# Causal attention on one core: the fourth key block of a chunk's diagonal joins the second one's tile of scores

## The reference, cut to what matters

```
def _L0_attn_ref(x, Wq, Wk, Wv, Wo, bo):        # x: (4, 2048, 256), 16 heads of 16
    q, k, v = split_heads(x @ Wq), split_heads(x @ Wk), split_heads(x @ Wv)
    scores = jnp.einsum('bhqd,bhkd->bhqk', q, k) * HEAD ** (-0.5)
    scores = jnp.where(causal, scores, -jnp.inf)
    weights = jax.nn.softmax(scores, axis=-1)
    out = jnp.einsum('bhqk,bhkd->bhqd', weights, v)
    return out.transpose(0, 2, 1, 3).reshape(B, S, N_EMBD) @ Wo + bo

x = x + _L0_attn_ref(_layernorm(x), ...)
x = x + _L0_ffn_ref(_layernorm(x), L0_ffn_rhs)   # rows quantised to int8, one 256x256 product
```

## Time and profile before

| | before |
|---|---|
| median of 3 executions | 1966.17 us (1963.51 to 1981.74) |
| profiled execution | 1967.51 us, span 1965.7 us |
| mean granted TensorE clock | 0.944 of full speed |
| PE busy | 1746.4 us, 89% of the span |
| DVE busy | 1503.5 us, 76% |
| ACT busy | 1406.9 us, 72% |
| POOL busy | 339.6 us, 17% |

### The profile page before, as it was taken

One profiled execution on the slowest core, in us unless ns is written; L12 is line 12 of the kernel. 1 busy time (PEld: TensorE's weight loads), 2 busy tenths in 40 slices (PEclk: granted clock), 3 DMA queues, 4 the chain that ended last, 5 costly groups with the idle time before them and its releaser, 6 DMA issues. The chain is left out here.

```text
span 1965.7 us, 43129 instructions
## 1 busy us (share of the span) xinstructions
PE 1746.4 (89%) x17855; PEld 676.0 (34%) x17855; DVE 1503.5 (76%) x1761; ACT 1406.9 (72%) x2915; POOL 339.6 (17%) x379
## 2 busy tenths in 40 slices
PE   5888888999999899999999999999999998887773
PEld 3444442333333333333333333333233332225442
DVE  3546558999979798988989798989789894106776
ACT  2222226888978888888888898888788888874443
POOL 7212210101010111111110101011111111013443
PEclk9989998999999999999999999999899998887876
DMA  3333220111110101010111111010101010403661
GB/s 100 123 107 105 84 68 22 29 31 41 29 38 21 43 16 43 23 36 30 29 30 38 34 30 42 16 43 16 43 28 30 30 29 19 141 18 105 187 203 63
DMA packets 102492, 106.36 MB, mean 54 GB/s; under 512 B 19092, under 2 KB 85912, under 8 KB 102296
## 3 DMA queue, kind: packets, MB, share of 16 engines
q1 hardware_dynamic: 102296, 103.60, 17.6%
HBM read 60.56 MB, written 42.47 MB: 52 GB/s over the span
## 5 line engine op out<-in xcount | busy, mean ns | idle before, releaser
L915 ACT ACTIVATE prob<-psum 128x512 f32<-128x512 f32 (+3 forms) x2560 | 1224.2, 532 | 214.0 <-PE psum L822 171.6
L346 DVE TENSOR_REDUCE pmax<-psum 128x2 f32<-128x1024 f32 (+1 forms) x960 | 1107.0, 1215 | 165.1 <-PE psum L259 128.0
L842 PE MATMUL psum<-prob,V 128*32 128x256 f32 (+1 forms) x10240 | 752.6, 367 | 9.9 <-ACT ust L904 7.2
L822 PE MATMUL psum<-Q,K 50*128 50x512 f16 (+3 forms) x2560 | 465.6, 359 | 50.9 <-ACT prob L915 40.9
L931 POOL TENSOR_SCALAR_AFFINE_SELECT prob<-prob 128x512 f32<-128x512 f32 x256 | 162.9, 636 | 1322.0 <-ACT prob L915 1322.0
L842 PEld LDWEIGHTS psum<-prob,V 128*32 128x32 f32 x10240 | 204.5, 109 | 331.2 <-issue 259.2
L259 PE MATMUL psum<-K,Q 48*128 48x512 f16 x1536 | 301.7, 395 | 13.2 <-DMA K<-k_parts 8.4
L822 PEld LDWEIGHTS psum<-Q,K 50*128 50x128 f16 x2560 | 125.7, 93 | 304.9 <-ACT prob L915 275.7
L259 PEld LDWEIGHTS psum<-K,Q 48*128 48x128 f16 x1536 | 72.3, 93 | 283.6 <-issue 159.7
L346 DVE TENSOR_REDUCE pblk<-psum 128x8 f32<-128x1024 f32 x128 | 152.2, 1217 | 8.9 <-PE psum L278 8.4
L278 PE MATMUL psum<-K,Q 48*128 48x512 f16 (+3 forms) x1024 | 126.8, 300 | 0.0
(11 more groups left out here) (104 smaller groups left out, 741.0 us busy)
## 6 DMA issues: line engine op xcount, KB each, us to landing
f_x<-in_L_attn_x SPq DMA_DIRECT2D x32, 512.0 KB, 3.9
unnormalised<-ust SPq DMA_DIRECT2D x64, 256.0 KB, 3.1
q_parts<-part SPq DMA_DIRECT2D x64, 128.0 KB
k_parts<-part SPq DMA_DIRECT2D x64, 128.0 KB
Q<-q_parts SPq DMA_DIRECT2D x128, 64.0 KB, 2.4
K<-k_parts SPq DMA_DIRECT2D x128, 64.0 KB, 2.0
f_us<-unnormalised SPq DMA_DIRECT2D x32, 256.0 KB
f_rs<-inverse_sums SPq DMA_DIRECT2D x32, 256.0 KB
```

The lines of the kernel that those rows point to most:

```text
L346: nc.vector.tensor_reduce(to, of, axis=AX.X, op=ALU.max).then_inc(mx_free, 1)
L822: nc.tensor.matmul(PS[:, SB + (i + half) % RING, 0:CH - lo], K[it % 2][rows, pair, kb * P:(kb + 1) * P], Q[it % 2][rows, pair, c * CH + lo ...
L842: m = nc.tensor.matmul(PS[32 * h:32 * h + 32, UB, cols], V[:, it // NG * NT + kb, col:col + 32], prob[(it * NSTEP + k) % PRING][:, h, cols ...
L915: nc.scalar.activation(prob[g % PRING][:, h, 0:n], PS[:, SB + i % RING, 0:n], ACT.Exp, scale=by).then_inc(exp_done, 1)
```

## The change

The second diagonal block of a chunk (384 queries) and the fourth (128 queries) now share one step and one tile of scores of 512 columns: columns 0 to 383 belong to key block 4c+1, columns 384 to 511 to key block 4c+3. Its pair of scores has four matmuls in the place of two, its exps have the full width, and POOL masks it twice, at column 0 and at column 384. The third diagonal block (256 queries) becomes the last step of its chunk. An iteration has 36 steps, 72 half-slots.

The values of diagonal steps are no longer halved: the shared step has one block of 384 columns and one of 128, the 256-wide step has a single block of 256 in slot 1 and none in slot 3. The full-width steps keep two blocks of 256.

`place_turns` has other costs: each block of values 0.145 and, new, `change` of 0.093 where values follow anything but values; 0.32 and 0.396 for the two sorts of diagonal turns, 0.15 for the turn `None`, 1.155 for DVE. The number of turns and their sequence stay as they were; their places among the slots are computed anew.

```
+def steps_of_iteration():
...
+    steps = []
+    for c in reversed(range(NCH)):
+        first = TPC * c
+        steps += [(c, [(kb, 0, CH)]) for kb in range(first + 1)]
+        steps += [(c, [(first + 1, 0, CH - P), (first + 3, CH - P, P)]), (c, [(first + 2, 0, CH // 2)])]
+    return steps
...
+def value_blocks(k):
...
+    _, parts = STEPS[k]
+    if parts[0][2] == CH:
+        return [(parts[0][0], at, at, CH // 2) for at in (0, CH // 2)]
+    return [(kb, at, CH - n, n) for kb, at, n in parts]
...
-    hop, land, mask, rows, block = 0.12, 0.27, 0.85, 6.0, 0.14
+    hop, land, mask, rows, block, change = 0.12, 0.27, 0.85, 6.0, 0.145, 0.093
...
-            pe = max(pe, free) + (0.08 if kind is None else 0.23 if kind[0] == "off" else 0.4)
-            vec = max(vec, pe + land) + (2.6 if kind is None else 1.17)
+            pe = max(pe, free) + (0.15 if kind is None else 0.226 if kind[0] == "off" else
+                                  0.32 if len(DIAG[kind[2]][1]) == 1 else 0.396)
+            vec = max(vec, pe + land) + (2.6 if kind is None else 1.155)
...
-                pe = max(pe, ready) + w * 2 / 2400 + block
+                pe = max(pe, ready) + wide * 4 / 2400 + block + (0.0 if after_values else change)
...
-                for half in range(2):
-                    rows = slice(half * HALF, half * HALF + SROWS)
-                    nc.tensor.matmul(PS[:, SB + (i + half) % RING, 0:CH - lo],
-                                     K[it % 2][rows, pair, kb * P:(kb + 1) * P],
-                                     Q[it % 2][rows, pair, c * CH + lo:(c + 1) * CH], start=True, stop=True
-                                     ).then_inc(s_ready, 1)
...
+                for j, (kb, at, n) in enumerate(parts):
+                    for half in range(2):
+                        rows = slice(half * HALF, half * HALF + SROWS)
+                        m = nc.tensor.matmul(PS[:, SB + (i + half) % RING, at:at + n],
+                                             K[it % 2][rows, pair, kb * P:(kb + 1) * P],
+                                             Q[it % 2][rows, pair, (c + 1) * CH - n:(c + 1) * CH], start=j == 0,
+                                             stop=j == len(parts) - 1, skip_group_check=True)
+                        if j == len(parts) - 1:
+                            m.then_inc(s_ready, 1)
...
-                for k, (c, kb) in enumerate(STEPS):
-                    if kb < TPC * c:
+                for k, (c, parts) in enumerate(STEPS):
+                    if parts[0][0] < TPC * c:
                         continue
                     pool.wait_ge(exp_done, it * NS + G * k + G)
-                    d = prob[(it * NSTEP + k) % PRING][:, :, 0:P]
-                    nc.gpsimd.affine_select(out=d, in_=d, compare_op=ALU.is_ge, fill=0.0, base=0,
-                                            pattern=[[0, G], [1, P]], channel_multiplier=-1).then_inc(masked, 1)
+                    for _, at, _ in parts:
+                        d = prob[(it * NSTEP + k) % PRING][:, :, at:at + P]
+                        nc.gpsimd.affine_select(out=d, in_=d, compare_op=ALU.is_ge, fill=0.0, base=0,
+                                                pattern=[[0, G], [1, P]], channel_multiplier=-1).then_inc(masked, 1)
```

More of the change, by code:

```diff
@@ L38 @@
 EXPONENT = 0x7F800000
-STEPS = [(c, kb) for c in reversed(range(NCH)) for kb in range(TPC * (c + 1))]
+def steps_of_iteration():
[5 more added lines that the diff above has]
+    return steps
+STEPS = steps_of_iteration()
 NSTEP = len(STEPS)
+WIDE = [sum(n for _, _, n in parts) for _, parts in STEPS]
+ON_DIAGONAL = [0, 1, 3, 2]
 LAG = 3
 PRING = 4
-def step_cols(c, kb):
-    return max(0, kb - TPC * c) * P
+def value_blocks(k):
[3 more added lines that the diff above has]
+    return [(kb, at, CH - n, n) for kb, at, n in parts]
 def kinds_of_iteration():
@@ L131, in place_turns @@
             if slot % 2 == 1:
-                if g < LAG:
+                v = g - LAG
+                if v < 0 or slot // 2 >= len(VALUES[v % NSTEP]):
                     continue
-                v = g - LAG
-                (c, kb), w = STEPS[v % NSTEP], wide[v % NSTEP]
-                ready = exp_at[v, G - 1] + hop + (mask if kb >= TPC * c else 0.0)
+                c, parts = STEPS[v % NSTEP]
+                kb, _, _, wide = VALUES[v % NSTEP][slot // 2]
+                ready = exp_at[v, G - 1] + hop
+                if kb >= TPC * c:
+                    ready += mask * (slot // 2 + 1 if len(parts) > 1 else 1)
                 if kb == 0 and v:
@@ L819, in scores, with values @@
                     pe.wait_ge(exp_done, i + 2 - RING)
-                for half in range(2):
-                    rows = slice(half * HALF, half * HALF + SROWS)
-                    nc.tensor.matmul(PS[:, SB + (i + half) % RING, 0:CH - lo],
-                                     K[it % 2][rows, pair, kb * P:(kb + 1) * P],
-                                     Q[it % 2][rows, pair, c * CH + lo:(c + 1) * CH], start=True, stop=True
-                                     ).then_inc(s_ready, 1)
-            def values(it, k, second):
-                c, kb = STEPS[k]
-                lo = step_cols(c, kb)
-                mid = (lo + CH) // 2
+                for j, (kb, at, n) in enumerate(parts):
[7 more added lines that the diff above has]
+                            m.then_inc(s_ready, 1)
+            def values(it, k, block):
+                c, parts = STEPS[k]
+                kb, at, to, n = VALUES[k][block]
                 ci = NCH - 1 - c
-                if not second:
+                if block == 0:
                     if kb == 0 and it * NCH + ci >= 1:
@@ L836, in values @@
                     pe.wait_ge(exp_done, it * NS + G * k + G)
-                    if kb >= TPC * c:
-                        pe.wait_ge(masked, it * NT + ci * TPC + kb - TPC * c + 1)
-                cols = slice(mid, CH) if second else slice(lo, mid)
+                if kb >= TPC * c and (block == 0 or len(parts) > 1):
+                    pe.wait_ge(masked, it * NT + ci * TPC + ON_DIAGONAL.index(kb - TPC * c) + 1)
                 for h in range(G):
                     col = VS * ((it % NG) * G + h)
-                    m = nc.tensor.matmul(PS[32 * h:32 * h + 32, UB, cols], V[:, it // NG * NT + kb, col:col + 32],
-                                         prob[(it * NSTEP + k) % PRING][:, h, cols.start - lo:cols.stop - lo],
-                                         start=kb == 0 and not second, stop=kb == TPC * (c + 1) - 1,
-                                         skip_group_check=True)
-                if second:
+                    m = nc.tensor.matmul(PS[32 * h:32 * h + 32, UB, to:to + n], V[:, it // NG * NT + kb, col:col + 32],
+                                         prob[(it * NSTEP + k) % PRING][:, h, at:at + n],
+                                         start=kb == 0 and block == 0, stop=k in ENDS, skip_group_check=True)
+                if block == len(VALUES[k]) - 1:
                     m.then_inc(p_free, 1)
@@ L883, in _ @@
                         if slot % 2 == 1:
-                            if g >= LAG:
-                                values((g - LAG) // NSTEP, (g - LAG) % NSTEP, slot == 3)
+                            if g >= LAG and slot // 2 < len(VALUES[(g - LAG) % NSTEP]):
+                                values((g - LAG) // NSTEP, (g - LAG) % NSTEP, slot // 2)
                             continue
@@ L890, in _ @@
             for k in range(NSTEP - LAG, NSTEP):
-                for second in (False, True):
-                    values(ITS - 1, k, second)
+                for block in range(len(VALUES[k])):
+                    values(ITS - 1, k, block)
         @block.scalar
```

23 lines of the change are left out of this document (13 added, 10 removed).

## The result

The changed kernel takes **1896.88 us** (median of 4 executions, 1889.54 to 1904.45) against 1965.06 (4 executions, 1963.51 to 1981.74): 68 us less, a ratio of 0.9635 with a 95% interval of 0.9564 to 0.9705. The forecast was 1896. Medians here are over all executions of a kernel, while ratios leave out those more than 1.5% above its fastest, so the two can differ (most for p3_before_dve_130, where that is five of ten).

What follows compares the result with a forecast made beforehand. A full-width half-slot costs the larger of PE's sum and 1.107 us, the pace of the ring of three score banks. 15 iterations at 4.5 us less plus 3.7 for the last make 71 us: 1896 us, range 1872 to 1938.

Steps and rivals of the forecast that it cites:

- The iteration: One iteration of `attend`, copy to copy: half-slots sum to 82.3 us against 86.9, 4.5 less, so near 86.3 us.
- The last iteration: Final iteration of `attend`, which has no turns: half-slots paced at 1.107 us, 3.7 us less than before.
- Turns: a turn put into an empty full-width half-slot costs almost nothing: PE's half-slots: 0.89 + 0.22 us against 1.107; 69 turns in 72 half-slots, not 80, those without a turn from 17 to 8.
- Values: 0.45 less and three switches: PE's narrow value blocks: 0.45 us less a chunk plus three switches into fp32 values, 0.3; some 3 us an iteration.
- Exps and scores: Shared tile: scores taken at 0.32 us; 4 fewer ACT calls, at most 0.47 us a chunk, with the gain in the ring.
- I leave the 4.0 us of other waits as they are: Waits per iteration beyond the half-slot sum (copy of UB, loads, DVE): 90.85 against 86.9 us, taken as unchanged.
- DVE: down to 6 us: DVE in an iteration: work unchanged at 80.2 us, idle time down to 6 us, off the path but only just.
- Masks cost nothing: Shared step's second mask, 0.64 us, covered by 3.8 us before its values; bound 0 to -0.3 a chunk, taken 0.
- A: Rival: only PE's sum counts, an iteration falls by PE's 3 us alone, 47 us in all, 1920; chance 0.13.
- B: Rival: DVE becomes the bound, the iteration falls by 2 us, 32 us in all, 1935; chance 0.11.
- D: Rival: PE and ring go by columns, not blocks or pairs, so no change, 1966; chance 0.05.
- C: Rival: turns closer to chunk loads block PE and scores; at 2 us each, 24 us longer, 1991; chance 0.04.

Runs made afterwards that it cites:

- p3_before_dve_130: The kernel before with one cost in place_turns raised, DVE's turn at 1.30 in place of 1.17: 1961.82 us, ratio 0.9898.
- y1: The changed kernel plus a zero-weight matmul of 512 columns in 142 half-slots, 34 of which do have a turn: 1912.8 us, ratio 0.9692.
- y3: The changed kernel with diagonal value blocks cut in two, back to back in the same slot, turn table unchanged: 1898.94 us, ratio 0.9631.
- x3: The changed kernel with diagonal values halved again, only the 256 block over two slots, turns placed anew: 1896.94 us, ratio 0.9684.
- q2: The changed kernel with diagonal values halved again and DVE's turn cost at 1.19 in place of 1.155: 1852.93 us, ratio 0.9443.
- x2: The kernel before, its 40 steps without shared tile, with the new costs and each narrow step's values in one block: 2007.23 us, ratio 1.0204.
- x4: The changed kernel with the costs of the kernel before in place_turns: 1861.25 us, ratio 0.9466.
- p1: The changed kernel with one cost in place_turns raised, DVE's turn at 1.2 in place of 1.155: 1864.93 us, ratio 0.9465.
- y2: The changed kernel with DVE's off-diagonal turns reducing 384 of each bank's 512 columns, turn table unchanged: 1901.74 us, ratio 0.9658.

## Why the prediction was right

The number was right, and most of its steps; two were wrong in what they rest on. That it came out to the microsecond is in part luck, as the first two points show.

- **The iteration.** Forecast 86.3, measured 86.8: with half-slots for 82.3 as summed, 4.5 would be other waits, where I left 4.0. The fall from iterations of before at full clock is some 3.5 us (90.3 to 86.8) and by the mean of 14 iterations 3.7, not 4.5. Over 15 iterations that makes 56 us in place of 67.
- **The last iteration.** Forecast 3.7 less, measured 10.2, since in the profiled execution of before some 25 us of it ran at the lower clock (0.86 in the earlier trace rows), and some 3 in that of after. At 1.98 us a half-slot these 22 us explain most of the 10, so how much of the 3.7 was there cannot be told. The term was right in its pace (1.15, 1.07, 1.14) and says nothing on the clock. It and the untouched phases fill up what the iterations lack, so that 71 us forecast and 68 measured agree better than their parts do.
- **"Turns: a turn put into an empty full-width half-slot costs almost nothing."** Held: 0.02 of 0.22 us where there is truly no turn (y1). So the lost half-slots are what the change gives back. The half-slots without a turn went from 15 to 9 by PE's order, where I counted 17 and some 8.
- **"Values: 0.45 less and three switches" a chunk.** This step failed. The fixed 0.15 us belongs to a run of values, not to a block (y3). For the table of before the sum is right all the same, since there the two halves stood in different slots, with scores between. But PE's time saved by the whole blocks is not seen as time saved in the iteration (x3 and q2, with the block of 256 divided: nothing; x2: a loss). The half-slots that it lightens are paced by the ring; one that is emptied falls no further than 1.107.
- **"Exps and scores".** The shared pair takes 0.32, and the gain lies in the ring, where eight half-slots an iteration vanish (x3: all of the gain).
- **"I leave the 4.0 us of other waits as they are."** They did stay in the sum, but this hid the largest thing in the case. 3 us an iteration can be had by the places of the turns alone (x4, p1), and the new costs do not take them. I had the table as given and priced the half-slots as if each turn stood well; nor has the sum a term for the clock, which costs the change some 19 us from 500 to 1600 us by the estimate above.
- **"DVE: down to 6 us" idle.** 7.4 measured (79.38 busy of 86.80); it is off the path (y2).
- **"Masks cost nothing."** No wait of the values (L872) for POOL stands among the waits after.
- **Rivals.** A, at 1920, lies outside the interval of the result, and x2 and x3 refute it; B is refuted by y2. D's rule, that a further block costs next to nothing, is right inside a run of values, and its conclusion that nothing changes is wrong, since the pairs of scores were never the same in number. C's waits are there, 9.1 us in 1100, the longest 1.3, but they were there before (8.2), so they could not turn the sign. They do stand before most falls of the clock, which C had not in it.

What stays open is what exactly makes the clock fall. It falls behind stretches in which PE does less (7.23 of 9.30 us before 0.54, 6.99 of 7.50 before 1.00), often with a wait of about 1 us in them, and over the whole loop the kernels with the least idle PE have the full clock. That is a correlation, with the exceptions named above, and no run has set PE's load there by itself. Open too is whether the whole blocks would bring anything against halves in separate slots once the turns are well placed: only x2 compares these, with its turns placed as early as before.

## What to carry to other kernels

Where a ring of few buffers sets a least time for each turn of it, count the turns of the ring, not the work: merging two narrow tiles into one full one removed turns and gave all of the gain here, while PE work saved inside a turn that the ring paces anyway gave nothing that the runs could show. When the shape of such a schedule changes, search again over the costs that place the side work, and measure: one number, 1.155 or 1.2, was worth 32 us here, half as much as the change itself. A stretch that leaves the matrix engine idle may be paid for twice, once by the idle time and once by the clock behind it, so look at both. And where a schedule is computed, see whether it is the same in every round: here one trace held good and bad places side by side, and could tell what the total could not.

## What the runs showed of the hardware

- A run of fp32 values between scores or turns costs about 0.15 us above the columns (1.67 ns each), once for the run, however many blocks are in it: 384 columns 0.785 us as one block, 0.790 as two of 192; 256 columns 0.571 and 0.576 as two of 128; 128 columns 0.358 and 0.363 as two of 64 (the change and y3_split_narrow, to the next turn).
- At the lower clock the ring slows as well: a half-slot takes 1.98 us in the place of 1.12. PE in order of time, the changed kernel, behind the copy at 1267.13:

```profile
1267.77 1.08 PE L872 MATMUL psum<-prob,V 128*32 128x256 f32 x8 [0.35 <-ACT ust L933]
...
1269.75 1.08 PE L872 MATMUL psum<-prob,V 128*32 128x256 f32 x8
```

  The blocks follow each other at 1.98 us, and DVE's turns with them. The 7.4 us of that stretch have the work of some 4.2.
- The clock that the profiled loop gets differs between versions that do the same work: 0.98 for the change, 1.00 for p1, which only places the turns otherwise.
- The clock can fall to the lower level behind waits of PE of about 1 us (six of 0.98 to 1.30 us in the change, each followed within 3 us; three of 1.07 to 1.43 in the kernel before, none followed). The longest gap of PE in the change from 400 to 1590 us is 1.3 us, and the clock fell eight times there.
